# Six attention layers over 128 graphs: new instruction orders around layer 0's result, for the first four groups and at the end

## The chip, the cores and the metric

One Trainium2 chip, of which one core runs the program. The time is device microseconds of one execution. The kernel before took 2340.16 us (median of three runs, 2338.4 to 2341.12); the execution that was profiled took 2338.19 us. Engines: PE is TensorE's matmul side and PEld its weight loads, DVE is VectorE, ACT is ScalarE, POOL is GpSimd, SP is SyncE, which here only issues DMAs.

## The reference

128 graphs of 128 nodes, 256 features a node, and a 0/1 adjacency matrix for each graph, go through six layers:

```python
# layer 0: eight heads of 32
q, k, v = x @ Wq + bq, x @ Wk + bk, x @ Wv + bv
attn = softmax(where(adj == 0, -inf, q @ k.T / sqrt(32)))
x = layernorm(x + (attn @ v) @ Wo + bo) * gamma + beta
# layer 1: one head of 256
attn = softmax(where(adj == 0, -inf, (x @ Wq) @ (x @ Wk).T / sqrt(256)))
x = layernorm(x + (attn @ (x @ Wv)) @ Wo + bo) * gamma + beta
# layers 2 to 5: one head, q and k of width 128
attn = softmax(where(adj == 0, -1e10, (x @ Wq.T + bq) @ (x @ Wk.T + bk).T / sqrt(128)))
x = layernorm(x + (where(adj == 0, 0, attn) @ x) @ Wc.T) * gamma + beta
```

All of it is float32. The output is x after layer 5.

## The kernel before

**Groups, items and slots.** Two graphs are a group; there are 64 groups. One layer (1 to 5) of one group is an item, and the items stand in numbered slots: slot 5g + 4(layer - 1) holds that layer of group g, so from slot 16 on each run of five slots holds one item of each layer, of five different groups. Slot i is written i16, i17 and so on, and a period is five slots. Layer 0 of a group is no item: its parts are spread over the slots ahead of the group's layer 1 by `due(i, lead)`, which gives the group whose layer 1 stands `lead` slots later. With lead 9, 8 and 7 its v, q and k are projected (`project_v0`, `project_q0`, `project_k0`); with 6 all scores are made (`score0`); with 6 to 3 the four units of two heads go through the row minimum (`row_max0`), the exponential (`exp0`), the reciprocal, the scaling on POOL (`normalise_probs0`), the transposing on PE and the move out of PSUM (`move_probs0T`); with 3 the heads are made (`heads0`), with 2 they are split (`move_headsT`, `split_headsT`) and joined (`join_heads`), and the residual and the statistics follow on DVE; with 1 the result is normalised. This result is called GROUP.

**Split operands.** A projection is three float32r products (high by high, high by low, low by high). So ACT writes the high half of a transposed x (`split_hi`), DVE the low half (`split_lo`), and only then can PE run `project_qk` of the item.

**An item.** PE: `transpose_x`, `project_qk`, `project_v` in two halves, `score`, and one slot later `transpose_probs`, two slots later `context`. ACT: `split_hi`, `move_qk`, `softmax`, `move_probsT`, `move_v`. DVE: `split_lo`, `row_max`, then `add_residual`, `statistics` and `normalise` (L1007, two TENSOR_SCALAR). POOL: `find_rstd` (L1172 and L1174), `scale` by gamma (L1190) and `shift` by beta (L1198), which writes the item's x. The first and last few results are `alone`: DVE makes them by itself in `centre` and `finish`, and POOL only gives the reciprocal deviation.

**What sets the order.** The kernel is raw: each engine has its own written program, a loop over the slots with the calls in a fixed order, and semaphores between the engines. Nothing reorders it. An instruction that waits holds all that stands behind it on its engine. ACT's `exp0` of one unit is four ACTIVATEs (L740). After slot 320 an order written out by hand runs the last five items (`LAST_ITEMS`; p, q, a, b, c, d, e are slots 319, 320, 321, 322, 324, 325, 327).

For the item of the layer before, the wait of `transpose_x` is `wait_result`, on `x_ready` (or `alone_ready`); for layer 1 it is GROUP's x. `score` waits for `qk_ready` and for the item before's `probsT_ready`.

## Time and profile before

| what | value |
|---|---|
| median of three runs | 2340.16 us |
| the profiled execution | 2338.19 us, of which its span 2336.4 us |
| PE busy | 2257.7 us, 97% of the span |
| PEld, DVE, ACT, POOL busy | 91%, 76%, 69%, 77% |
| mean granted TensorE clock | 0.994 |

A busy share is an average over stages. Here there are three: the filling of the pipeline (slots -12 to about 15, the first 140 us), the steady part in which a period comes 59 times, and the draining from about 2220 us on. A time in the rows is from the span's start. "Idle before" in brackets is the time the engine stood still before that instruction, with what ended it. PE's own ends are modelled, so two matmuls overlap by some tenths in the rows: a hole in PE is read from the starts, as a distance that is longer than the same distance where nothing waits.

### The profile page before, as it was taken

The numbers are of one execution on the slowest core, as the hardware profiler recorded it, in microseconds if no ns is written. First come the engines' busy times: TensorE is split into PE (matmuls) and PEld (weight loads), VectorE is DVE, ScalarE is ACT, GpSimd is POOL, SyncE is SP. The second block draws the span as 40 slices with busy tenths as digits, with TensorE's granted clock in tenths as the row PEclk, the third lists the DMA queues.
The fourth block names the chain that finished last, engine by engine and source line by source line (L and its number), as shares of the span: only waits on it lengthen the run. The fifth ranks groups of instructions, "written<-read, shape, count | busy, mean of one in ns | idle before, by whom it ended". The sixth has DMA issues, their size and how long they took to land.

```text
span 2336.4 us, 59698 instructions
## 1 busy us (share of the span) xinstructions
PE 2257.7 (97%) x20624; PEld 2132.9 (91%) x20624; DVE 1771.6 (76%) x7736; ACT 1614.4 (69%) x5515; POOL 1787.6 (77%) x2397
## 2 busy tenths in 40 slices
PE   6899999999999999999999999999999999999986
PEld 5799999999999999999999999999999999999985
DVE  4777877877877877777777777777778778777776
ACT  5667767767767767767767767767677677677653
POOL 3368878878878878878788788788788788788762
PEclk9999999999999999999999999999999999999998
DMA  4000110110110110010010100100100100000000
GB/s 157 20 24 24 31 29 24 31 29 24 31 29 24 30 30 24 27 33 22 29 31 24 28 29 26 29 28 27 28 29 26 29 27 28 29 25 26 11 15 14
DMA packets 38747, 68.78 MB, mean 29 GB/s; under 512 B 4400, under 2 KB 12848, under 8 KB 37936
## 3 DMA queue, kind: packets, MB, share of 16 engines
q1 hardware_dynamic: 38448, 64.97, 9.2%
q8 instruction: 166, 2.72, 0.5%
q14 instruction: 133, 1.09, 0.2%
HBM read 48.18 MB, written 16.78 MB: 28 GB/s over the span
## 4 chain that ended last, share of the span: by engine, by line
PE 78%; DVE 9%; ACT 8%; issue 2%; POOL 2%; DMA 0%; POOLq 0%; SPq 0%; DVEq 0%
PE value_bank L464 17%; PE qk_bank L456 16%; PE context_bank L619 9%; PE unit_bank L464 8%; PE unit_bank L456 7%; PE score_bank L603 5%; PE qk_bank L569 5%; ACT probs L740 5%; PE unit_bank L523 5%; PE unit_bank L535 3%; PE score_bank L600 2%; DVE scores L919 2%; PE score_bank L610 2%; DVE xT_lo L948 2%; DVE scores L954 1%
## 5 line engine op out<-in xcount | busy, mean ns | idle before, releaser
L1190 POOL TENSOR_TENSOR x<-y,rows 128x512 f32<-128x512 f32 x304 | 390.3, 1284 | 188.5 <-DVE y L1007 188.5
L740 ACT ACTIVATE probs<-scores,negmax 128x128 f32<-128x128 f32 x1024 | 400.8, 400 | 88.9 <-DVE negmax L919 88.9
L1007 DVE TENSOR_SCALAR y<-y,mv,rstd 128x256 f32<-128x256 f32 x728 | 299.4, 453 | 175.7 <-POOL rstd L1174 175.5
L456 PE MATMUL qk_bank<-xT_hi,w_lo 128*128 128x256 f32 x1280 | 414.9, 324 | 17.0 <-DVE xT_lo L948 13.0
L1198 POOL TENSOR_TENSOR x<-x,rows 128x512 f32<-128x512 f32 x304 | 392.5, 1291 | 19.1
L762 ACT CAST xT_hi<-qk_bank 128x512 fp32r<-128x512 f32 x257 | 150.1, 584 | 355.0 <-PE qk_bank L569 354.9
L464 PE MATMUL value_bank<-w_lo,xT_hi 128*128 128x256 f32 x1280 | 393.7, 308 | 0.0
L456 PE MATMUL qk_bank<-xT_lo,w_hi 128*128 128x256 f32 x1280 | 362.5, 283 | 0.0
L456 PE MATMUL qk_bank<-xT_hi,w_hi 128*128 128x256 f32 x1280 | 360.8, 282 | 0.0
L464 PE MATMUL value_bank<-w_hi,xT_lo 128*128 128x256 f32 x1280 | 360.8, 282 | 0.0
L464 PE MATMUL value_bank<-w_hi,xT_hi 128*128 128x256 f32 x1280 | 358.8, 280 | 0.0
L988 DVE SCALAR_TENSOR_TENSOR y<-context_bank,rtotal,x 128x256 f32<-128x256 f32 x640 | 279.3, 478 | 95.0 <-PE context_bank L619 94.6
L619 PE MATMUL context_bank<-v,probsT 128*128 128x256 f32 x1280 | 336.5, 385 | 1.7 <-ACT probsT L794 1.7
L1179 POOL TENSOR_TENSOR probs<-probs,rtotal 128x256 f32<-128x256 f32 x512 | 307.2, 621 | 37.6 <-DVE rtotal L938 37.6
L788 ACT ACTIVATE probs<-scores,negmax 128x128 f32<-128x128 f32 x640 | 254.4, 404 | 65.7 <-DVE negmax L954 65.6
L1174 POOL TENSOR_TENSOR rstd<-var_eps,minus_half 128x2 f32<-128x2 f32 x384 | 273.0, 711 | 32.0
L456 PEld LDWEIGHTS qk_bank<-xT_hi,w_lo 128*128 128x128 f32 x1280 | 242.5, 189 | 49.7 <-DVE xT_lo L948 37.8
L954 DVE CUSTOM_DVE_ANT_0 scores<-score_bank,mask 128x128 f32<-128x128 f32 x640 | 160.4, 289 | 167.4 <-PE score_bank L603 147.6
L996 DVE BATCH_NORM_STATS2 bn<-y 128x6 f32<-128x256 f32 x768 | 285.6, 414 | 0.0
L456 PEld LDWEIGHTS qk_bank<-xT_hi,w_hi 128*128 128x128 f32 x1280 | 243.2, 190 | 4.8
L464 PEld LDWEIGHTS value_bank<-w_hi,xT_hi 128*128 128x128 f32 x1280 | 243.3, 190 | 0.1
L619 PEld LDWEIGHTS context_bank<-v,probsT 128*128 128x128 f32 x1280 | 218.6, 190 | 26.8 <-ACT probsT L794 2.4
(98 smaller groups left out, 6532.7 us busy)
## 6 DMA issues: line engine op xcount, KB each, us to landing
x0T<-xT_in SPq DMA_DIRECT2D x64, 256.0 KB, 3.0
x<-x_in SPq DMA_DIRECT2D x64, 256.0 KB, 3.1
out<-x_out SPq DMA_DIRECT2D x64, 256.0 KB, 2.3
adj<-adj_in SPq DMA_DIRECT2D x64, 128.0 KB, 2.2
late_weights<-w_in SPq DMA_DIRECT2D x2, 1024.0 KB, 7.3
rows<-rows_in SPq DMA_DIRECT2D x1, 1792.0 KB, 11.6
probs0T<-w_in SPq DMA_DIRECT2D x4, 256.0 KB, 4.1
x<-w_in SPq DMA_DIRECT2D x1, 1024.0 KB, 13.1
```

The lines of the kernel that those rows point to most:

```text
L456: mm = pe.matmul(psum[:, n * G * N:(n + 1) * G * N], split(w, name, kd, at, at + P), flat(xT_half[:, kd]), start=kd == 0 and w is w_lo, st ...
L464: mm = pe.matmul(psum[:, g * D:(g + 1) * D], xT_half[:, kd, g], split(w, name, kd), start=kd == 0 and w is w_lo, stop=kd == KD - 1 and xT_ ...
L619: mm = pe.matmul(context_bank[:, g * D:(g + 1) * D], probsT[:, ring(i), g], v[:, ring(i), g], start=True, stop=True)
L740: e = act.activation(probs0[:, j, g, quad], scores0[:, j, g, quad], ACT.Exp, scale=-1.0, bias=negmax0[:, j, g, quad:quad + 1], accum_out=t ...
L788: e = act.activation(probs[:, ring(i), g], scores[:, ring(i), g], ACT.Exp, scale=-1.0, bias=negmax[:, small(i), g:g + 1], accum_out=total[ ...
L988: dve.scalar_tensor_tensor(y[:, r, g], psum[:, g * D:(g + 1) * D], factor[:, g:g + 1], kept[:, g], ALU.mult, ALU.add).then_inc(y_ready, 1)
L996: last = note(dve.bn_stats(bn[:, r, g], y[:, r, g]))
L1007: m = dve.tensor_scalar(y[:, r, g], y[:, r, g], mv[:, r, g, 0:1], rstd[:, r, g:g + 1], ALU.subtract, ALU.mult)
L1174: pool.tensor_tensor(rstd[:, r], var_eps[:, r], minus_half[:, :], ALU.pow).then_inc(rstd_ready, 1)
L1179: m = pool.tensor_tensor(probs0[:, j, g], probs0[:, j, g], rtotal0[:, j, g].unsqueeze(2).to_broadcast([P, QUADS, N]), ALU.mult)
L1190: pool.tensor_tensor(result(norm), y[:, NORM_AT[norm] % YS], row_of_each(f"gamma{layer}"), ALU.mult).then_inc(zg_ready, 1)
L1198: pool.tensor_tensor(result(norm), result(norm), row_of_each(f"beta{layer}"), ALU.add).then_inc(x_ready, 1)
```

## The change

Seven things are moved or split; apart from how one unit's exponentials are issued (in two halves), no arithmetic is added or removed.

1. DVE, all periods: in the slots with `due(i, 1)` and `due(i, 0)` (i19 and i20, say), the item's `row_max` stands behind `split_lo` (and in the first of them behind GROUP's `normalise`) and not ahead of it.
2. DVE, slot with `due(i, 2)` (i18): GROUP's `add_residual` and `statistics` stand ahead of the normalising of item i-2 and not behind it. POOL, same slot: `find_rstd` of GROUP stands ahead of `scale` of item i-2.
3. ACT: the unit 0 of `exp0` is issued in two halves, the first graph in slot i19, the second at the start of i20.
4. Groups 0 to 3 (`early`): PE makes `transpose_probs0(3)` and `heads0` ahead of the next group's q, and `join_heads` ahead of the next group's k; ACT makes `exp0(2)` and `exp0(3)` a step sooner, ahead of `move_qk`; DVE and POOL follow; the normalising of the item in that slot stands behind `split_headsT`; GROUP's `centre` and `finish` get `row_max0(0)` between them.
5. The fused weights of layer 1 are split one slot later.
6. From i316 on: `score` stands in its own slot, and `context` one slot sooner, behind it.
7. In the order at the end: `transpose_x(e)` ahead of `project_v(d, 0)`, `row_max(e)` ahead of `add_residual(d)`, both last results centred before either is finished, and some neighbours swapped.

```diff
 def scored_early(i):
-    return not item(i + 1) or i >= LAST_FIRST + 3
+    return not item(i + 1) or i > LAST_FIRST
+
+def context_early(i):
+    return i > LAST_FIRST
+
+def early(group):
+    return 0 <= group < 4
...
@@ tensor @@
-                if (group := due(i, 8)) is not None:
+                if (group := due(i, 3)) is not None and early(group):
+                    transpose_probs0(group, 3)
+                if (group := due(i, 8)) is not None and not early(group - 1):
                     project_q0(group)
-                if (group := due(i, 7)) is not None:
+                if (group := due(i, 7)) is not None and not early(group - 1):
                     project_k0(group)
-                if item(i - 2):
+                if item(i - 2) and not context_early(i - 2):
                     context(i - 2)
+                if (group := due(i, 3)) is not None and early(group):
+                    heads0(group)
+                if (group := due(i, 8)) is not None and early(group - 1):
+                    project_q0(group)
                 if item(i):
                     project_qk(i)
...
                 if (group := due(i, 2)) is not None:
                     join_heads(group)
+                if (group := due(i, 7)) is not None and early(group - 1):
+                    project_k0(group)
...
                 if item(i) and scored_early(i):
                     score(i)
+                if item(i - 1) and context_early(i - 1):
+                    context(i - 1)
                 if item(i) and not late_values(i):
                     project_v(i, 1)
...
+            transpose_x(e)
             project_v(d, 0)
-            transpose_x(e)
             score(d)
...
@@ scalar @@
                 if item(i):
                     split_hi(i)
+                if (group := due(i, 5)) is not None and item(i - 1):
+                    exp0(group, 0, [1])
...
                 if (group := due(i, 3)) is not None:
                     move_probs0T(group, 2)
+                    if early(group):
+                        move_probs0T(group, 3)
...
-                if (group := due(i, 6)) is not None:
-                    exp0(group, 0)
+                if (group := due(i, 6)) is not None and not early(group):
+                    exp0(group, 0, [0] if item(i) else range(G))
                 if (group := due(i, 5)) is not None:
                     exp0(group, 1)
+                    if early(group):
+                        exp0(group, 2)
...
@@ vector @@
-                if item(i - 1):
+                urgent = due(i, 1) is not None or due(i, 0) is not None
+                if item(i - 1) and not urgent:
                     row_max(i - 1)
+                if item(i - 2) and context_early(i - 2):
+                    add_residual(("item", i - 2))
                 if item(i):
                     split_lo(i)
-                if (group := due(i, 1)) is not None:
-                    finish_or_normalise(("group", group))
+                if (group := due(i, 1)) is not None and ("group", group) not in ALONE_AT:
+                    normalise(("group", group))
+                if item(i - 1) and urgent:
+                    row_max(i - 1)
                 if (group := due(i, 2)) is not None:
                     split_headsT(group)
+                    if item(i - 3) and early(group):
+                        finish_or_normalise(("item", i - 3))
+                if (group := due(i, 1)) is not None and ("group", group) in ALONE_AT:
+                    centred = centre(("group", group))
                 if (group := due(i, 6)) is not None:
                     row_max0(group, 0)
+                if (group := due(i, 1)) is not None and ("group", group) in ALONE_AT:
+                    finish(("group", group), centred)
...
-                if item(i - 2):
-                    finish_or_normalise(("item", i - 2))
                 if (group := due(i, 2)) is not None:
                     add_residual(("group", group))
                     statistics(("group", group))
+                if item(i - 2) and not (due(i, 3) is not None and early(due(i, 3))):
+                    finish_or_normalise(("item", i - 2))
...
             reciprocal_total(d)
+            row_max(e)
             add_residual(("item", d))
-            row_max(e)
...
@@ gpsimd @@
                 if item(i - 1):
                     keep_valid(i - 1)
+                if (group := due(i, 2)) is not None:
+                    find_rstd(("group", group))
                 if item(i - 2):
                     scale(("item", i - 2))
...
                 if (group := due(i, 2)) is not None:
-                    find_rstd(("group", group))
                     scale(("group", group))
                     shift(("group", group))
```

Three places show how the instructions stand. The first is DVE from GROUP's residual to GROUP's normalising (i18 and the start of i19) in the steady part, before. L988 on `unit_bank` is GROUP's residual, L1007 the normalising (first of item i16, then of GROUP), L954 is `row_max`, L948 `split_lo`.

```order
L1007 TENSOR_SCALAR y<-y,mv,rstd 128x256 x2
L988 SCALAR_TENSOR_TENSOR y<-unit_bank,rvalid,x 128x256 x2
L996 BN_STATS bn<-y 128x6 x2
L999 BN_AGGR mv<-bn 128x2 x2
L954 ISA scores,negmax<-score_bank,mask 128x128
L954 ISA negmax 128x1
L954 ISA scores,negmax<-score_bank,mask 128x128
L954 ISA negmax 128x1
L948 TENSOR_TENSOR xT_lo<-qk_bank,xT_hi 128x512
L1007 TENSOR_SCALAR y<-y,mv,rstd 128x256 x2
```

The same place after the change, where the line numbers are 30 higher:

```order
L1018 SCALAR_TENSOR_TENSOR y<-unit_bank,rvalid,x 128x256 x2
L1026 BN_STATS bn<-y 128x6 x2
L1029 BN_AGGR mv<-bn 128x2 x2
L1037 TENSOR_SCALAR y<-y,mv,rstd 128x256 x2
L978 TENSOR_TENSOR xT_lo<-qk_bank,xT_hi 128x512
L1037 TENSOR_SCALAR y<-y,mv,rstd 128x256 x2
L984 ISA scores,negmax<-score_bank,mask 128x128
L984 ISA negmax 128x1
L984 ISA scores,negmax<-score_bank,mask 128x128
L984 ISA negmax 128x1
```

GROUP's residual and statistics went to the front, the row minimum to the back.

The second is DVE at the step from i19 to i20, before: the normalising of item i17, `row_max` of i19, `split_lo` of i20 (on `unit_bank`), and the first reciprocal of unit 0.

```order
L1007 TENSOR_SCALAR y<-y,mv,rstd 128x256 x2
L954 ISA scores,negmax<-score_bank,mask 128x128
L954 ISA negmax 128x1
L954 ISA scores,negmax<-score_bank,mask 128x128
L954 ISA negmax 128x1
L948 TENSOR_TENSOR xT_lo<-unit_bank,xT_hi 128x512
L938 RECIPROCAL rtotal<-total 128x4
```

And after:

```order
L1037 TENSOR_SCALAR y<-y,mv,rstd 128x256 x2
L978 TENSOR_TENSOR xT_lo<-unit_bank,xT_hi 128x512
L984 ISA scores,negmax<-score_bank,mask 128x128
L984 ISA negmax 128x1
L984 ISA scores,negmax<-score_bank,mask 128x128
L984 ISA negmax 128x1
L968 RECIPROCAL rtotal<-total 128x4
```

`split_lo` stands between item i17's normalising and the row minimum of i19.

The third is POOL in i18 and the start of i19, before. L1172 and L1174 are `find_rstd`, L1190 `scale`, L1198 `shift`; `x_out` is written for an item of layer 5.

```order
L1172 TENSOR_SCALAR var_eps<-mv 128x2
L1174 TENSOR_TENSOR rstd<-var_eps,minus_half 128x2
L1165 TENSOR_TENSOR rtotal<-rtotal,valid 128x2
L1190 TENSOR_TENSOR x_out<-y,rows 128x512
L1172 TENSOR_SCALAR var_eps<-mv 128x2
L1174 TENSOR_TENSOR rstd<-var_eps,minus_half 128x2
L1190 TENSOR_TENSOR x<-y,rows 128x512
L1198 TENSOR_TENSOR x<-x,rows 128x512
```

And after, with line numbers 48 higher:

```order
L1220 TENSOR_SCALAR var_eps<-mv 128x2
L1222 TENSOR_TENSOR rstd<-var_eps,minus_half 128x2
L1213 TENSOR_TENSOR rtotal<-rtotal,valid 128x2
L1220 TENSOR_SCALAR var_eps<-mv 128x2
L1222 TENSOR_TENSOR rstd<-var_eps,minus_half 128x2
L1238 TENSOR_TENSOR x_out<-y,rows 128x512
L1238 TENSOR_TENSOR x<-y,rows 128x512
L1246 TENSOR_TENSOR x<-x,rows 128x512
```

The scaling of item i16 now stands between GROUP's reciprocal deviation and GROUP's own scaling.

## Rows read from the trace of the kernel before

**Rows 1.** The page: busy tenths of PE in 40 slices.

```profile
PE   6899999999999999999999999999999999999986
```

**Rows 2.** Windows: stretch; length; busy of PE, PEld, DVE, ACT, POOL; clock; DMA.

```profile
140.52:175.74 35.22, 34.89 (x324) 33.13 (x324) 26.77 (x123) 25.07 (x87) 27.43 (x38) 1.00 0.08 20
...
2196.00:2336.40 140.40, 116.05 (x903) 103.66 (x902) 97.64 (x368) 69.67 (x219) 68.13 (x102) 0.96 0.03 12
```

**Rows 3.** Waits of PEld, 140 to 2196 us: total, times, longest.

```profile
PEld unit_bank L569 <- POOL x L1198: 19.1, 58, 0.3
PEld qk_bank L456 <- DVE xT_lo L948: 18.9, 59, 1.2
```

**Rows 4.** Timeline of PE, one period: start, us, instruction, idle before.

```profile
165.16 0.28 PE L464 MATMUL unit_bank<-w_hi,headsT_lo 128*128 128x256 f32 x1
...
172.19 0.28 PE L464 MATMUL value_bank<-w_hi,xT_lo 128*128 128x256 f32 x1
172.60 0.66 PE L569 MATMUL unit_bank<-eye,x 128*128 128x128 f32 x4
173.46 0.68 PE L603 MATMUL score_bank<-kT,qT 128*128 128x128 f32 x4 [0.20 <-ACT probsT L794]
...
181.75 0.39 PE L456 MATMUL qk_bank<-xT_hi,w_lo 128*128 128x256 f32 x1
```

**Rows 5.** Timeline of DVE, same period.

```profile
166.19 0.87 DVE L988 SCALAR_TENSOR_TENSOR y<-unit_bank,rvalid,x 128x256 f32<-128x256 f32 x2
...
173.55 0.74 DVE L1007 TENSOR_SCALAR y<-y,mv,rstd 128x256 f32<-128x256 f32 x2 [0.36 <-POOL rstd L1174]
174.20 0.29 DVE L954 CUSTOM_DVE_ANT_0 scores<-score_bank,mask 128x128 f32<-128x128 f32 x1
...
174.62 0.69 DVE L948 TENSOR_TENSOR xT_lo<-unit_bank,xT_hi 128x512 fp32r<-128x512 f32 x1
```

**Rows 6.** Timeline of POOL, same period.

```profile
166.35 1.28 POOL L1190 TENSOR_TENSOR x_out<-y,rows 128x512 f32<-128x512 f32 x1 [0.69 <-DVE y L1007]
168.03 0.22 POOL L1172 TENSOR_SCALAR var_eps<-mv 128x2 f32<-128x2 f32 x1 [0.39 <-DVE mv L999]
168.32 0.71 POOL L1174 TENSOR_TENSOR rstd<-var_eps,minus_half 128x2 f32<-128x2 f32 x1
...
171.26 1.29 POOL L1198 TENSOR_TENSOR x<-x,rows 128x512 f32<-128x512 f32 x1
```

**Rows 7.** Timeline of ACT, same period.

```profile
167.56 0.59 ACT L762 CAST xT_hi<-qk_bank 128x512 fp32r<-128x512 f32 x1 [1.49 <-PE qk_bank L569]
...
174.74 0.40 ACT L788 ACTIVATE probs<-scores,negmax 128x128 f32<-128x128 f32 x1 [0.86 <-DVE negmax L954]
...
180.31 0.58 ACT L762 CAST xT_hi<-qk_bank 128x512 fp32r<-128x512 f32 x1
```

**Rows 8.** Timelines of DVE, POOL and PE where a normalising met a POOL instruction.

```profile
425.99 2.11 DVE L1007 TENSOR_SCALAR y<-y,mv,rstd 128x256 f32<-128x256 f32 x2
...
429.18 0.39 PE L456 MATMUL qk_bank<-xT_hi,w_lo 128*128 128x256 f32 x1 [0.81 <-DVE xT_lo L948]
...
2256.40 1.68 DVE L1007 TENSOR_SCALAR y<-y,mv,rstd 128x256 f32<-128x256 f32 x2 [1.08 <-POOL rstd L1174]
...
2256.33 1.28 POOL L1198 TENSOR_TENSOR x_out<-x_out,rows 128x512 f32<-128x512 f32 x1
```

**Rows 9.** Timelines of PE and ACT while the pipeline fills.

```profile
26.02 0.84 ACT L725 ACTIVATE q0T<-unit_bank,cols 128x256 f32<-128x256 f32 x2 [0.82 <-PE unit_bank L456]
...
73.68 1.13 PE L600 MATMUL score_bank<-xT,qT 128*128 128x128 f32 x8 [1.00 <-ACT probsT L794]
...
89.69 0.39 PE L456 MATMUL qk_bank<-xT_hi,w_lo 128*128 128x256 f32 x1 [2.66 <-DVE xT_lo L948]
```

**Rows 10.** Timeline of PE while it drains.

```profile
2282.08 1.03 PE L619 MATMUL context_bank<-v,probsT 128*128 128x256 f32 x4
2283.64 0.39 PE L456 MATMUL qk_bank<-xT_hi,w_lo 128*128 128x256 f32 x1 [0.54 <-DVE xT_lo L948]
```

More of the change, by code:

```diff
@@ L645, in _ @@
                     project_v0(group)
-                if (group := due(i, 3)) is not None:
+                if (group := due(i, 3)) is not None and not early(group):
                     transpose_probs0(group, 3)
@@ L661, in _ @@
                     transpose_probs0(group, 2)
-                if (group := due(i, 3)) is not None:
+                if (group := due(i, 3)) is not None and not early(group):
                     heads0(group)
@@ L670, in _ @@
             p, q, a, b, c, d, e = LAST_ITEMS
-            context(p)
             project_qk(a)
@@ L734, in move_k0, with exp0 @@
                 m.then_inc(k0_ready, 1)
-            def exp0(group, j):
+            def exp0(group, j, graphs=range(G)):
                 act.wait_ge(negmax0_ready, after_unit(group, j))
-                for g in range(G):
+                for g in graphs:
                     for quad in range(QUADS):
@@ L742, in exp0 @@
                                            accum_out=total0[:, j, g, quad:quad + 1])
-                e.then_inc(exp0_ready, 1)
+                if g == G - 1:
+                    e.then_inc(exp0_ready, 1)
             def move_probs0T(group, j):
@@ L829, in _ @@
                     move_v(i - 1)
-                if (group := due(i, 6)) is not None:
-                    exp0(group, 0)
+                if (group := due(i, 6)) is not None and not early(group):
+                    exp0(group, 0, [0] if item(i) else range(G))
                 if (group := due(i, 5)) is not None:
                     exp0(group, 1)
+                    if early(group):
+                        exp0(group, 2)
                 if (group := due(i, 4)) is not None:
                     move_probs0T(group, 1)
-                    exp0(group, 3)
+                    if not early(group):
+                        exp0(group, 3)
                 if (group := due(i, 8)) is not None:
@@ L844, in _ @@
                     move_probsT(i - 1)
+                if (group := due(i, 6)) is not None and early(group):
+                    exp0(group, 0, [0] if item(i) else range(G))
                 if (group := due(i, 5)) is not None:
-                    exp0(group, 2)
-                if (group := due(i, 3)) is not None:
+                    exp0(group, 3 if early(group) else 2)
+                if (group := due(i, 3)) is not None and not early(group):
                     move_probs0T(group, 3)
-                if i == -5:
+                if i == -4:
                     split_fused(0)
@@ L862, in _ @@
             move_v(a)
+            move_probsT(a)
             split_hi(b)
-            move_probsT(a)
             move_qk(b)
@@ L1072, in _ @@
                     reciprocal0(group, 2)
+                    if early(group):
+                        reciprocal0(group, 3)
                 if item(i - 1) and item(i - 1)[0] == 1:
@@ L1075, in _ @@
                 if item(i - 2):
-                    add_residual(("item", i - 2))
+                    if not context_early(i - 2):
+                        add_residual(("item", i - 2))
                     statistics(("item", i - 2))
@@ L1088, in _ @@
                     find_valid(group)
-                    reciprocal0(group, 3)
+                    if not early(group):
+                        reciprocal0(group, 3)
                 if (group := due(i, 8)) is not None:
                     make_mask(group)
-                if item(i - 2):
-                    finish_or_normalise(("item", i - 2))
                 if (group := due(i, 2)) is not None:
@@ L1107, in _ @@
             row_max(q)
+            add_residual(("item", p))
             split_lo(a)
-            add_residual(("item", p))
             statistics(("item", p))
@@ L1119, in _ @@
             statistics(("item", a))
-            centred = centre(("item", a))
+            normalise_alone(("item", a))
             row_max(b)
-            finish(("item", a), centred)
             split_lo(c)
@@ L1137, in _ @@
             reciprocal_total(d)
+            row_max(e)
             add_residual(("item", d))
-            row_max(e)
             statistics(("item", d))
             reciprocal_total(e)
-            normalise_alone(("item", d))
+            centred_d = centre(("item", d))
             add_residual(("item", e))
             statistics(("item", e))
-            normalise_alone(("item", e))
+            centred_e = centre(("item", e))
+            finish(("item", d), centred_d)
+            finish(("item", e), centred_e)
         @block.gpsimd
@@ L1205, in _ @@
                     normalise_probs0(group, 2)
+                    if early(group):
+                        normalise_probs0(group, 3)
                 if (group := due(i, 3)) is not None:
-                    normalise_probs0(group, 3)
+                    if not early(group):
+                        normalise_probs0(group, 3)
                     make_residual0(group)
```

2 lines of the change are left out of this document (1 added, 1 removed).

## The prediction

> **What bounds the kernel now.** I read the page first. PE is busy in nine tenths of nearly every slice; the holes are in the first three slices and the last one or two [rows 1]. So PE's stream sets the time, and an order can win only PE's idle time. The windows say how much there is: one steady period takes 35.22 us, and the last 140.4 us hold 116.05 us of PE's work, so 24 us of holes [rows 2]. In the steady part the page shows no hole, since matmul ends are modelled; the waits of PEld do. Twice in each of 58 or 59 periods its weight load waits, for x from POOL (19.1 us in all) and for xT_lo from DVE (18.9 us) [rows 3]. The timeline of one period (GROUP 4, items i16 to i21) gives the places, read by starts:
>
> A. The last product ahead of the transpose starts at 172.19, and the next could follow 0.12 later, at 172.31; `transpose_x(i20)` starts at 172.60, because it waits for GROUP's x, whose shift on POOL ran from 171.26 to 172.55 [rows 4, 6]. A hole of 0.29.
> B. `score(i19)` starts 0.86 after that transpose; four transposes take 0.43 where nothing waits. It waits for ACT, which ran unit 0's exponentials ahead of the move. A hole of 0.43.
> C. `project_qk(i21)` at 181.75 waits for `split_lo(i21)`, which waits for `split_hi(i21)` on ACT at 180.31 [rows 4, 7]. By PEld's waits 18.9 / 59 = 0.3.
>
> Together 1.0 us a period, some 59 us in all. Behind C is a chain that I take for the real bound of a period: POOL's deviation of i17, DVE's normalising of i17 (173.55), `row_max(i19)` (174.20), `softmax(i19)` on ACT (174.74), then ACT without a break up to `split_hi(i21)` (180.31), `split_lo`, `project_qk(i21)` [rows 5, 7]. The trace has one test of it: at 425.99 that stretch's normalising took 2.11 us in place of some 1.24, `split_lo` came late, and PE lost 0.81 us at 429.18 in place of 0.3 [rows 8]. What comes late in that chain costs PE its full length.
>
> **The steady part.** Nothing on PE moves. I follow the same period with the new orders.
>
> On DVE, GROUP's residual can start 0.32 after the last join product (165.16, so 165.48; elsewhere in the trace this distance is 0.31 to 0.32) in place of 166.19 [rows 4, 5]. With its statistics it takes 1.75, so it is through at 167.23, not 167.93; i16's normalising follows and ends as late as the old block did, at 167.9. `split_lo(i19)` needs ACT's high half (167.56 + 0.59 = 168.15 [rows 7]), so it runs from 168.2 to 168.85, and GROUP's normalising could start there (before: 169.07).
>
> On POOL, GROUP's `find_rstd` takes 1.0 (168.03 to 168.32 + 0.71) and would end at about 168.3, and now `scale(i16)` follows at once, for 1.28 us, up to 169.6 [rows 6]. GROUP's normalising comes at 168.85 in the middle of it. What happens then is in the trace: at 2256.40 a pair of the same instruction began 0.07 after a POOL instruction of 1.28 us and took 1.68 in place of 0.74 [rows 8]. The longest single one took 1.36. The DVE instruction stood until POOL's was over. So GROUP's normalising ends at about 170.2, not 169.5. POOL's `scale` and `shift` of GROUP then need 2.65, and x is there at 172.9: hole A grows from 0.29 to 0.6.
>
> The Trainium skill has this as a rule (SBUF — State Buffer, section Who interferes with whom): DVE's two-port modes, which `tensor_scalar` can enter, and GpSimd share one pair of ports, and "whoever issues first gets the shared pair for the whole instruction". The trace agrees. By the rule the collision is certain here, since POOL issues first; without it the period would lengthen by 0.6 only, as under the first rival.
>
> Then the chain. All that DVE does after GROUP's normalising is 0.7 later than before (the order inside it costs nothing), so i17's statistics, its deviation and its normalising come 0.7 later: 174.25. Behind it stands now `split_lo(i20)` with a step of 0.65 ahead of `row_max(i19)`, which comes at 174.25 + 0.65 + 0.65 = 175.5 in place of 174.20. So 1.3 later; `softmax(i19)` and ACT's unbroken run keep the 1.3. The two exponentials that moved to the start of i20 lie in ACT's 0.86 of idle time before that softmax and cost nothing; if that cover were gone they would cost 0.8. Hole B shrinks from 0.43 to about 0.1, since only half a unit stands ahead of `move_qk`: but the PE time it frees is given back at C, because the chain does not start from PE. `project_qk(i21)` starts at 183.05, and the period takes 36.5. Behind C nothing else is near: ACT's and DVE's next steps have idle time before them.
>
> Bounds. Below: without the port collision i17's normalising stays at 173.6, `split_lo(i20)` alone shifts `row_max(i19)`, 0.6 a period. The second bound needs more: even with everything else on time, `split_lo(i20)` waits for `transpose_x(i20)` at 172.31 and ACT's half behind it (0.69 + 0.63), so it starts at 173.63 and `row_max(i19)` 0.61 later, at 174.24, as late as now: 0.0. Above: POOL's short `find_rstd` of GROUP meets the two instructions of i16's normalising and loses 0.4, so 1.7. I take 1.3, the value from the row at 2256.40, as the periods are alike. It holds for 59 periods: 59 x 1.3 = +77 us (0.6: +35; 1.7: +100).
>
> **Filling the pipeline (groups 0 to 3).** Gains: normalising items behind `split_headsT` and `split_lo` takes away the waits for xT_lo, 2.66 at 89.69 and one like it a period on (1.96), and the join of group 1 waited 2.24 behind such a `finish`; the first of the three stands in [rows 9]. Together 6.9. Losses: (a) `exp0(2)` stands ahead of `move_qk` of the layer-1 item; `score` of that item waits for ACT already (1.00 at 73.68), and a unit takes 1.55, in groups 1, 2 and 3, of which the sooner `row_max` gives back about half: 2.5. (b) `move_headsT` stands on ACT behind `move_q0`, whose q is now projected behind `heads0`: 1.4 of projection and 0.84 of move [rows 9] before the join can begin, in groups 0 and 1: 2.2 each, of which k's projection had filled 1.5 before. 3.0 in all. Net about -1. Longer holes can also drop PE's clock, which was at its lower level (1.2 GHz) four times in this stretch, each time behind a hole of 2 to 4 us; one more costs about 1.7. Range -7 to +8.
>
> **Draining.** `context` filled PE between the next item's transpose and its projection. That distance is set by ACT's and DVE's halves (2.0 us from the transpose; the context at 2282.08 lay inside it, and `project_qk` at 2283.64 waited all the same) [rows 10]. Now it lies behind `score`, so each of five slots is longer by its 0.67: +3.4. Two slots also take `score` in, with a wait for probsT of 0.5 and its own 0.44 out of the same gap: +1.9. `transpose_x(e)` waits for qk_bank: +0.4. `row_max(e)` a residual sooner: -1.3, and a wait of 0.7 for an x goes. Sum +3.7, range 0 to +8. The fused weights a slot later and the swaps inside this order cost nothing: other work covers them.
>
> **The sum**, against the profiled execution's 2338.2: -1 + 77 + 3.7 = 2417.9; the median of the runs is 2.0 above that execution, so 2420.
>
> **The rivals.**
> 1. *The ports do not collide.* For: some normalisings beside a short POOL instruction were not slowed. Against: the rows at 425.99 and 2256.40. Then 0.6 a period: 2338.2 + 35 + 2.7 + 2 = 2378. Chance 0.17.
> 2. *The other side: A and B shrink and nothing takes their place.* Place: `score(i19)` and `transpose_x(i20)`; price: A 0.25 and B 0.33, 0.58 a period, -34 us; with the ends as above 2309. It decides from the point at which softmax(i19) comes less than 0.3 later, measured from the transpose, than now. For: B is what the split of `exp0` frees, and the page's own waits name A and B. Against: ACT is unbroken from 174.74 to 180.31, and 425.99. Chance 0.12.
> 3. *A draw*: the new order of `row_max` and `split_lo` costs what A and B give, the bound 0.0 above. Then 2338.2 + 2.7 + 2 = 2343. Chance 0.06.
>
> **How the numbers follow.** My forecast (1.3 a period, between 1.0 and 1.7) has 0.65: own range 2395 to 2446. Range: 2368 to 2446, which takes in the first rival and leaves out the other two. A measurement of this kernel tells about 0.2% (4.7 us) from no change. Faster 0.13 (the second rival and a little of the third), same 0.05, slower 0.82.
>
> **What would show it.** Right: a period near 36.5 us by the starts of `score0`; pairs of L1037 (GROUP's) of 1.4 us or more in place of 0.74, beginning inside POOL's L1238 on `x_out`; `project_qk` of the layer-5 item waiting over 1 us for xT_lo, and `score` of the layer-2 item 0.1 or less for probsT; PE's clock unchanged at 1.00 in this part. Wrong: a period of 35.2 or less, or GROUP's normalising undisturbed (first rival if the period is 35.8).

## The result, and the profile after

The changed kernel took 2441.37 us (median of six runs, 2438.95 to 2445.76) against 2340.09 of the kernel before in the same set: ratio 1.0435, 95% interval 1.0421 to 1.0448. It is slower, by 4.4%. The forecast was 2420, own range 2395 to 2446. The profiled span is 2437.1 us against 2336.4.

First the page of the kernel after: span, busy time, busy tenths of PE, granted clock, the chain that ended last.

```profile
span 2437.1 us, 59698 instructions
PE 2306.4 (95%) x20624; PEld 2134.4 (88%) x20624; DVE 1812.7 (74%) x7736; ACT 1622.4 (67%) x5515; POOL 1791.5 (74%) x2397
...
PE   6899999999999999999999999999999999999986
...
PEclk9999999999999999999999999999999999999999
...
PE 56%; POOL 20%; DVE 17%; ACT 4%; issue 2%; DMA 0%; DVEq 0%; POOLq 0%; SPq 0%
```

PE still shows nines [rows 1], so the loss is not seen there; it is seen in the chain, which was 78% PE before, and in the windows: the period from `score0` of group 5 to that of group 6, and the draining (columns as in [rows 2]).

```profile
170.78:207.66 36.88, 35.74 (x323) 33.22 (x322) 27.86 (x120) 25.15 (x87) 28.68 (x39) 1.00 0.09 26
2309.62:2437.13 127.51, 99.62 (x753) 87.35 (x752) 90.23 (x332) 60.41 (x194) 58.72 (x88) 0.97 0.04 13
```

A period takes 36.88 us in place of 35.24 (means over 52 periods, groups 6 to 57), at a clock of 1.00. By the starts of `score0`: group 5 comes 2.9 us late, groups 5 to 63 take 95.2 us more (58 x 1.64), the rest 2.7 more. 2.9 + 95.2 + 2.7 = 100.8, the difference of the spans. So the loss is in the period.

Waits of PEld, 140 to 2190 us, answering [rows 3] (total, times, longest):

```profile
PEld qk_bank L466 <- DVE xT_lo L978: 68.3, 112, 1.2
PEld value_bank L474 <- ACT v L803: 34.3, 56, 0.6
PEld unit_bank L579 <- POOL x L1246: 24.5, 55, 0.5
```

The wait for xT_lo comes twice a period now, and there is a new one, of `project_v` for ACT's move of v. The same period as in [rows 4 to 7], PE:

```profile
175.79 0.66 PE L579 MATMUL unit_bank<-eye,x 128*128 128x128 f32 x4 [0.24 <-POOL x L1246]
176.31 0.68 PE L613 MATMUL score_bank<-kT,qT 128*128 128x128 f32 x4
...
180.74 0.39 PE L474 MATMUL value_bank<-w_lo,xT_hi 128*128 128x256 f32 x1 [0.36 <-ACT v L803]
...
186.22 0.39 PE L466 MATMUL qk_bank<-xT_hi,w_lo 128*128 128x256 f32 x1 [0.53 <-DVE xT_lo L978]
```

`score0` stands 2.88 later than before here; take that off every time. `transpose_x(i20)` then comes 0.31 later than in [rows 4], `score(i19)` 0.03 sooner, `project_qk(i21)` 1.59 later. DVE, POOL and ACT:

```profile
168.35 0.88 DVE L1018 SCALAR_TENSOR_TENSOR y<-unit_bank,rvalid,x 128x256 f32<-128x256 f32 x2 [1.03 <-PE unit_bank L474]
...
171.66 1.34 DVE L1037 TENSOR_SCALAR y<-y,mv,rstd 128x256 f32<-128x256 f32 x2
...
177.06 0.74 DVE L1037 TENSOR_SCALAR y<-y,mv,rstd 128x256 f32<-128x256 f32 x2 [0.25 <-POOL rstd L1222]
177.72 0.69 DVE L978 TENSOR_TENSOR xT_lo<-unit_bank,xT_hi 128x512 fp32r<-128x512 f32 x1
178.32 0.28 DVE L984 CUSTOM_DVE_ANT_0 scores<-score_bank,mask 128x128 f32<-128x128 f32 x1
...
183.24 1.91 DVE L1037 TENSOR_SCALAR y<-y,mv,rstd 128x256 f32<-128x256 f32 x2
...
185.48 0.68 DVE L978 TENSOR_TENSOR xT_lo<-qk_bank,xT_hi 128x512 fp32r<-128x512 f32 x1
```

```profile
171.27 1.27 POOL L1238 TENSOR_TENSOR x_out<-y,rows 128x512 f32<-128x512 f32 x1
...
182.53 1.18 POOL L1227 TENSOR_TENSOR probs<-probs,rtotal 128x256 f32<-128x256 f32 x2
183.67 1.32 POOL L1246 TENSOR_TENSOR x_out<-x_out,rows 128x512 f32<-128x512 f32 x1
```

```profile
178.85 0.40 ACT L808 ACTIVATE probs<-scores,negmax 128x128 f32<-128x128 f32 x1 [1.01 <-DVE negmax L984]
...
184.42 0.58 ACT L782 CAST xT_hi<-qk_bank 128x512 fp32r<-128x512 f32 x1
```

GROUP's pair starts 0.39 into POOL's `scale` of x_out and ends 0.46 behind it. `row_max(i19)` comes at 178.32, 1.24 late; `softmax(i19)` and ACT's unbroken run keep that up to `split_hi(i21)`. And then the pair of item i18 takes 1.91 us. Before, it was this, against these two steps of POOL:

```profile
179.13 1.24 DVE L1007 TENSOR_SCALAR y<-y,mv,rstd 128x256 f32<-128x256 f32 x2
```

```profile
178.99 1.23 POOL L1179 TENSOR_TENSOR probs<-probs,rtotal 128x256 f32<-128x256 f32 x2
180.18 1.31 POOL L1198 TENSOR_TENSOR x_out<-x_out,rows 128x512 f32<-128x512 f32 x1
```

That pair was over 0.19 after the `shift` of x_out began. In the kernel after the pair started 1.23 later, while POOL stood only 0.61 later, and its second half stood for the whole `shift`: it began at 13.00 after `score0`, 0.11 into the `shift`, and ended at 14.37, 0.15 behind it.

### The profile page after: what moved, and what is told of

Its sections match the earlier page's. It is cut to its first block, busy times and chain, and to the rows that moved or that the text cites. A ratio compares the mean times of both kernels' runs of the same rounds, so it can differ in the third digit from the quotient of the medians.

```text
span 2437.1 us, 59698 instructions
## 1 busy us (share of the span) xinstructions
PE 2306.4 (95%) x20624; PEld 2134.4 (88%) x20624; DVE 1812.7 (74%) x7736; ACT 1622.4 (67%) x5515; POOL 1791.5 (74%) x2397
## 4 chain that ended last, share of the span: by engine, by line
PE 56%; POOL 20%; DVE 17%; ACT 4%; issue 2%; DMA 0%; DVEq 0%; POOLq 0%; SPq 0%
PE qk_bank L466 12%; PE value_bank L474 11%; PE unit_bank L474 8%; PE unit_bank L466 7%; POOL probs L1227 6%; DVE y L1037 5%; PE context_bank L629 5%; PE qk_bank L579 4%; POOL rstd L1222 4%; POOL x L1238 3%; POOL x L1246 3%; POOL x_out L1246 3%; DVE xT_lo L978 3%; PE unit_bank L545 3%; PE score_bank L613 2%
## 5 line engine op out<-in xcount | busy, mean ns | idle before, releaser
L466 PE MATMUL qk_bank<-xT_hi,w_lo 128*128 128x256 f32 x1280 | 409.3, 320 | 48.4 <-DVE xT_lo L978 46.0
L1037 DVE TENSOR_SCALAR y<-y,mv,rstd 128x256 f32<-128x256 f32 x728 | 370.3, 550 | 75.7 <-POOL rstd L1222 75.7
L1220 POOL TENSOR_SCALAR var_eps<-mv 128x2 f32<-128x2 f32 x384 | 90.8, 237 | 271.0 <-DVE mv L1029 270.8
L474 PEld LDWEIGHTS value_bank<-w_lo,xT_hi 128*128 128x128 f32 x1280 | 242.7, 190 | 38.7 <-ACT v L803 38.5
```

What stands on the lines that cost most here:

```text
L466: mm = pe.matmul(psum[:, n * G * N:(n + 1) * G * N], split(w, name, kd, at, at + P), flat(xT_half[:, kd]), start=kd == 0 and w is w_lo, st ...
L474: mm = pe.matmul(psum[:, g * D:(g + 1) * D], xT_half[:, kd, g], split(w, name, kd), start=kd == 0 and w is w_lo, stop=kd == KD - 1 and xT_ ...
L1037: m = dve.tensor_scalar(y[:, r, g], y[:, r, g], mv[:, r, g, 0:1], rstd[:, r, g:g + 1], ALU.subtract, ALU.mult)
```

## The experiments

Every kernel keeps the period's order on PE, so means over the same 52 periods can be set side by side. All are worked out from the traces, in us after the start of `score0`; "pair" is start / duration of a normalising. The kernel before measured 2337.67 to 2340.52 us in the sets of runs, so a difference in us between kernels of two sets can be off by 3; periods do not have this.

| kernel | period | GROUP's pair | normalising i17 | row_max(i19) | pair of i18 | split_lo(i21) | project_qk(i21) |
|---|---|---|---|---|---|---|---|
| before | 35.24 | 1.18 / 0.74 | 5.66 | 6.31 | 11.25 / 1.25 | 13.14 | 13.89 |
| after | 36.88 | 0.89 / 1.35 | 6.29 | 7.54 | 12.48 / 1.89 | 14.72 | 15.45 |
| b_part2 | 35.55 | 1.14 / 1.10 | 5.99 | 6.64 | 11.58 / 1.25 | 13.47 | 14.21 |
| b_part1 | 36.55 | 1.18 / 0.73 | 5.98 | 7.23 | 12.16 / 1.90 | 14.40 | 15.14 |
| a_due0 | 35.83 | 0.89 / 1.35 | 6.29 | 6.95 | 11.88 / 1.24 | 13.70 | 14.44 |
| c_xout | 36.41 | 0.89 / 1.35 | 6.30 | 7.55 | 12.49 / 0.93 | 14.26 | 15.00 |
| a_nolock | 37.09 | 0.89 / 1.55 | 6.50 | 7.75 | 12.69 / 1.89 | 14.92 | 15.66 |
| c_rest | 35.16 | 1.17 / 0.74 | 5.66 | 6.31 | 11.25 / 1.24 | 13.06 | 13.80 |
| e_best | 34.57 | other form | 4.06 | 5.66 | 11.11 / 1.20 | 12.48 | 13.22 |

The periods of the five others are 35.23 (b_fill), 35.45 (d_form), 35.52 (d_orders), 35.51 (d_pair) and 35.94 (d_ts).

**Part 2 alone** (b_part2), on the kernel before:

```diff
@@ DVE; POOL likewise: find_rstd of GROUP ahead of scale of item i-2 @@
+                if (group := due(i, 2)) is not None:
+                    add_residual(("group", group))
+                    statistics(("group", group))
                 if item(i - 2):
                     finish_or_normalise(("item", i - 2))
```

> The kernel before, with part 2 alone: on DVE GROUP's residual and statistics ahead of the normalising of item i-2, on POOL find_rstd of GROUP ahead of scale of item i-2. row_max(i18) and split_lo(i19) stay ahead of GROUP's normalising, so it starts at 1.2 after score0 and POOL's scale runs up to 1.8. Theory: the pair takes 1.1 to 1.2 in place of 0.74, and the chain behind it comes 0.4 later, with 0.1 more by the second collision: 0.4 to 0.5 a period, 59 x 0.45 = +27, near 2367 us. Rival (no collision): 2335 to 2340.

2357.16 us, ratio 1.0074 (1.0059 to 1.0089); 0.31 a period. DVE and POOL:

```profile
171.92 1.10 DVE L1007 TENSOR_SCALAR y<-y,mv,rstd 128x256 f32<-128x256 f32 x2
```

```profile
171.28 1.28 POOL L1190 TENSOR_TENSOR x_out<-y,rows 128x512 f32<-128x512 f32 x1
```

The pair starts 0.25 later than in the kernel after and ends at the same moment, 0.46 behind POOL: its length is set by POOL's end. So part 2 loses by the collision it makes, though not the second one (1.25 as before), and less than expected.

**Part 1 alone** (b_part1), on the kernel before:

```diff
-                if item(i - 1):
+                urgent = due(i, 1) is not None or due(i, 0) is not None
+                if item(i - 1) and not urgent:
                     row_max(i - 1)
...
                     finish_or_normalise(("group", group))
+                if item(i - 1) and urgent:
+                    row_max(i - 1)
```

> The kernel before, with part 1 alone: row_max behind split_lo (and behind GROUP's normalising) in the slots with due(i, 1) and due(i, 0). Theory: row_max(i19) comes 0.6 later than before, and item i18's normalising meets POOL's shift of x_out as it does in the kernel after (pair 1.9 in place of 1.25 us): 0.6 + 0.3 = 0.9 a period, 59 x 0.9 = +53, near 2393 us (0.6 alone: 2375). softmax(i18) comes 1.8 later and with it the move of qk: hole B grows from 0.43 to about 1, without a price of its own. Rival (only the blocked normalising costs, the order is free): 2340. Rival (both holes B and C are paid): 2425.

2415.90 us, ratio 1.0326 (1.0309 to 1.0343); 1.31 a period, more than expected: GROUP's pair is undisturbed and still the normalising of i17 comes 0.32 late. `row_max(i18)` had used time in which DVE waited for GROUP's deviation; now it comes on top. 1.31 and 0.31 make 1.62 of the 1.64: the rest of the change has next to no price in the period.

**After, with half of part 1 undone** (a_due0):

```diff
-                urgent = due(i, 1) is not None or due(i, 0) is not None
+                urgent = due(i, 1) is not None
```

> The kernel after, with the row minimum of the item ahead of split_lo again in the slots with due(i, 0) (row_max(i19) ahead of split_lo(i20)); all else as after. Measured: 36.88 us a period against 35.24 before, of which project_qk(i21) is 1.56 late counted from score0. Theory (the late chain is GROUP's blocked normalising 0.63, split_lo ahead of the row minimum 0.61, and a longer second collision at item i18's normalising 0.3): the 0.61 goes, and perhaps 0.1 of the collision, 0.6 to 0.7 a period: 59 x 0.65 = -38 us, near 2403 us, with row_max(i19) at 6.9 after score0 in place of 7.54. Rival (PE waits for ACT, which the split exponentials hold up; the new wait of project_v for v): no change, 2441. Rival (this order is the whole of the loss): back to about 2345.

2379.76 us, ratio to before 1.0171 (1.0156 to 1.0186): 61.6 us back where 38 were expected. `row_max(i19)` is 0.59 sooner as computed, but the pair of i18 falls from 1.89 to 1.24 as well, and `project_qk(i21)` is 1.01 sooner. I had this collision down as a part of 0.1.

**The second collision by itself** (c_xout), on the kernel after:

```diff
@@ POOL (and the list of results in the same order) @@
-                if item(i - 4) and item(i - 4)[0] == LAYERS - 1:
-                    shift(("item", i - 4))
...
                     shift(("item", i - 2))
+                if item(i - 4) and item(i - 4)[0] == LAYERS - 1:
+                    shift(("item", i - 4))
```

> The kernel after, with POOL's shift of a layer-5 result (x_out) behind the scale and shift of the slot's other item instead of ahead of them; nothing else moved. It tests the second collision, the pair of item i18's normalising that takes 1.89 us from 12.48 after score0 and ends 0.16 behind that shift (12.89 to 14.21). Theory (that pair stands behind the shift of x_out and so makes row_max(i20) and split_lo(i21) late): the pair takes 1.1 to 1.3, project_qk(i21) comes 0.4 to 0.5 sooner, 36.4 a period, near 2414 us. Rival (ACT's unbroken run alone sets project_qk(i21)): the pair gets shorter, the period stays 36.9, 2441 us.

2413.58 us, ratio to before 1.0326 (1.0311 to 1.0342): 27.8 us back. DVE's pair of i18 in the same period:

```profile
183.72 0.95 DVE L1037 TENSOR_SCALAR y<-y,mv,rstd 128x256 f32<-128x256 f32 x2
```

Nothing of DVE, ACT or PE was reordered, `row_max(i19)` stands where it stood (7.55), and the period is 0.47 shorter. So 0.47 of the 1.64 hung on one POOL instruction.

**The first collision by another form** (a_nolock), on the kernel after, for GROUP alone:

```diff
@@ DVE, still behind the wait for rstd @@
-  dve.tensor_scalar(y, y, mean, rstd, subtract, mult)
+  dve.scalar_tensor_tensor(y, y, mean, gamma, subtract, mult)
@@ POOL @@
-  pool.tensor_tensor(x, y, gamma, mult)
+  pool.tensor_tensor(x, y, rstd broadcast, mult)
```

> The kernel after, with GROUP's normalising on DVE as a SCALAR_TENSOR_TENSOR, (y - mean) * gamma, that waits for the same semaphore as now, and POOL's scale multiplying by the reciprocal deviation instead of gamma; the order of everything is that of after. Theory (the pair takes 1.35 us because a TENSOR_SCALAR of DVE stands while POOL's scale of the item runs): a pair of SCALAR_TENSOR_TENSOR takes 0.87 wherever the trace has one and does not stand, so the pair takes 0.9, the chain behind it comes 0.45 to 0.5 sooner, 59 x 0.48 = -28 us, near 2413 us. Rival (the ports do not collide, the pair is long for another reason): the pair stays at 1.3 or more, 2441 to 2450 us.

2454.99 us, ratio to before 1.0492 (1.0476 to 1.0507): 13.6 us slower than the kernel after, and my premise was false.

```profile
172.41 1.54 DVE L1043 SCALAR_TENSOR_TENSOR y<-y,mv,rows 128x256 f32<-128x256 f32 x2
```

```profile
172.01 1.27 POOL L1250 TENSOR_TENSOR x_out<-y,rows 128x512 f32<-128x512 f32 x1
174.03 1.04 POOL L1250 TENSOR_TENSOR x<-y,rstd 128x512 f32<-128x512 f32 x1 [0.76 <-DVE y L1043]
```

This form stands for POOL too. The pairs of 0.87 that I had looked at read one operand from PSUM (`context_bank`, `unit_bank`); this one reads both from SBUF. The Trainium skill says it (SBUF — State Buffer, section Who interferes with whom): a DVE instruction with two SBUF inputs contends with a GpSimd instruction that reads SBUF. The trace agrees. The run's numbers (a pair of 1.3 or more, no faster than after) are those that I had given the rival, so by itself it does not tell the two apart; b_part2 and c_xout do.

**Parts 3 to 7 alone** (c_rest): after, with parts 1 and 2 undone.

```diff
-                if item(i - 1) and not urgent:
+                if item(i - 1):
                     row_max(i - 1)
...
-                if (group := due(i, 2)) is not None:
-                    find_rstd(("group", group))
                 if item(i - 2):
                     scale(("item", i - 2))
```

> The kernel after with parts 1 and 2 undone, so parts 3 to 7 alone (unit 0's exponentials in halves, the first four groups, the end). By the runs so far parts 1 and 2 cost 1.31 and 0.31 us a period apart and 1.64 together. Theory: part 3 shortens hole B by 0.34 and C gives it back, since ACT's chain does not start from PE: a period of 35.2, and the ends cost what the two traces showed, +1.5 in the filling and +2.7 in the draining: near 2344 us (2338 to 2350). Rival (a hole that shrinks is won: PE's order is bound by the sum of its holes): 34.9 a period, 2324 us. Rival (the split exponentials hold ACT up, which is what project_v's new wait for v shows): 35.5 a period or more, 2360.

2339.39 us, ratio 1.0011 (1.0002 to 1.0020), less than the 0.2% that a measurement of this kernel tells from no change. Hole B is gone from PEld's waits (23.7 us in 58 times for ACT's kT before), and this is where it went:

```profile
PEld qk_bank L466 <- DVE xT_lo L978: 47.6, 118, 1.3
```

In place of 18.6 us in 58 times it waits twice a period. `score(i19)` comes 0.37 sooner, `project_qk(i20)` at 7.47 as before: its `split_lo(i20)` stands behind `row_max(i19)` and the normalising of i17, which wait for POOL. B is given back, and already at `project_qk(i20)`, not at C.

**Parts 4 and 5 alone** (b_fill), on the kernel before: the lines of the change's diff with `early`, GROUP's `centre` and `finish` for results that are alone, and the fused weights a slot later.

```diff
+                if (group := due(i, 3)) is not None and early(group):
+                    transpose_probs0(group, 3)
...
+                if (group := due(i, 3)) is not None and early(group):
+                    heads0(group)
+                if (group := due(i, 8)) is not None and early(group - 1):
+                    project_q0(group)
```

> The kernel before with parts 4 and 5 alone (the orders of the first four groups, fused weights a slot later). The steady part and the end are those of before. Theory of the prediction: -1 us in all (2337); what the traces with parts 4 and 5 show so far is score0 of group 5 at 170.8 to 174.7 us against 167.9 to 170.8 in those without, so +1 to +5: near 2341 us. Rival (a gain as the shorter waits for xT_lo suggest): 2333.

2339.49 us, ratio 1.0005 (0.9996 to 1.0014): no change. PEld's longest wait for xT_lo up to 170 us stays at 2.8 (2.9 before); PE waits 4.3 us for `split_headsT` (headsT_lo) in place of 2.2, as loss (b) had it. PE's waits for xT_lo in this stretch are 6.8 us in 5 in place of 5.3 in 4, so the gain that was forecast for them is not there.

**A version that follows the chain** (d_form, d_orders, d_pair, d_ts, e_best). If POOL's deviation is what the chain waits for, DVE should not wait for it: the form of a_nolock for every result that is not alone, with a wait for the statistics only. First the form alone, then with part 3 and two orders (GROUP's normalising right behind its statistics; `row_max0(1)` behind `split_lo` of i20):

```diff
@@ d_form: normalise, scale @@
-                dve.wait_ge(rstd_ready, at + 1)
+                dve.wait_ge(stats_ready, at + 1)
...
+                pool.wait_ge(rstd_ready, NORM_AT[norm] + 1)
@@ d_orders, besides: DVE @@
                     statistics(("group", group))
+                    if ("group", group) not in ALONE_AT:
+                        normalise(("group", group))
```

> The kernel before, all orders kept, with every normalising that is not alone in another form: DVE makes (y - mean) * gamma (SCALAR_TENSOR_TENSOR, with a wait for the statistics and none for the reciprocal deviation), POOL multiplies by the reciprocal deviation and adds beta. Theory (POOL's deviation is what makes GROUP's x and the normalising of i17 late): GROUP's residual starts 0.6 sooner, since the item's step ahead of it no longer waits; POOL's scale with a broadcast factor takes 1.04 in place of 1.29 (measured in the first set), x of GROUP is there 0.2 to 0.3 sooner; period 35.0, near 2325 us (2300 to 2345). Rival (the new form stands behind POOL's instructions as TENSOR_SCALAR does, and more often since it comes sooner): 2340 or slower.

2349.93 us, ratio 1.0055 (1.0039 to 1.0072). Hole A halves (`transpose_x(i20)` at 4.56, not 4.70), but unit 0's `row_max0` comes 0.10 later, hole B grows by 0.24 (1.10 from transpose to score in place of 0.86), and the pair of i18 stands longer (1.47).

> The same new form of normalising on the kernel before, with part 3 (unit 0's exponentials in halves) and two orders on DVE: GROUP's (y - mean) * gamma right behind its statistics, ahead of row_max and split_lo of the next slot, and row_max0 of unit 1 behind split_lo of the next slot, so that it is not ahead of row_max(i19). Theory: GROUP's x is there 1 us or more sooner (hole A gone), row_max(i19) starts when score(i19) ends (B down by 0.34), project_qk(i21) 0.3 to 0.5 sooner (C gone): a period of 34.4 to 34.6, near 2296 us (2285 to 2320). Rival (collisions of the new form with POOL take it back): 2335 to 2350.

2352.82 us, ratio 1.0068 (1.0053 to 1.0083). `row_max(i19)` at 5.66 and holes A and C gone, as expected, and a new hole eats it, 0.93 us by the starts:

```profile
182.25 0.66 PE L523 MATMUL unit_bank<-eye,probs 128*128 128x128 f32 x4 [0.77 <-POOL probs L1187]
```

**d_pair** put `reciprocal0(0)` ahead of `row_max0(1)`, `split_lo(i21)` ahead of `row_max(i20)`, and x_out's shift later as in c_xout; **d_ts** is the same in the old form, with GROUP's normalising where it was. DVE:

```diff
-                if item(i - 1):
+                if item(i - 1) and not (item(i) and due(i, 4) is not None):
                     row_max(i - 1)
                 if item(i):
                     split_lo(i)
+                if item(i - 1) and item(i) and due(i, 4) is not None:
+                    row_max(i - 1)
...
                     reciprocal0(group, 0)
+                    if item(i - 1):
+                        row_max0(group, 1)
                     row_max0(group, 2)
```

> The kernel with the new form of normalising and its orders (d_orders: 35.52 us a period) with three more orders. Its trace shows the holes A and C gone and one new of 0.93 us, where transpose_probs0 of unit 1 waits for POOL's normalise_probs0, which had waited for the reciprocal of unit 0 that stood on DVE behind row_max0 of unit 1. So: reciprocal0(0) ahead of row_max0(1); split_lo(i21) ahead of row_max(i20); POOL's shift of x_out behind the slot's other scale and shift. Theory: the new hole goes, a period of 34.6 to 34.9 (A, B and C as good as gone), near 2310 us (2295 to 2325). Rival (ACT's unbroken run still sets project_qk(i21), whatever the order on DVE): 35.3 or more, 2340.

2351.41 us, ratio 1.0056 (1.0042 to 1.0070), with a period of 35.51, in the rival's range but not for its reason: the hole stayed at 0.93. I had named the wrong waiter. POOL:

```profile
178.60 0.22 POOL L1182 TENSOR_SCALAR var_eps<-mv 128x2 f32<-128x2 f32 x1 [0.91 <-DVE mv L1002]
...
179.58 1.50 POOL L1189 TENSOR_TENSOR probs<-probs,rtotal 128x256 f32<-128x256 f32 x2
```

`normalise_probs0(1)` stands behind `find_rstd(i18)`, whose statistics stand on DVE behind two `row_max0`.

> The kernel before with its own form of normalising (TENSOR_SCALAR with the reciprocal deviation) and the same orders as far as they apply: unit 0's exponentials in halves, row_max0(1) behind reciprocal0(0) in the next slot, split_lo(i21) ahead of row_max(i20), POOL's shift of x_out later. It tells what the orders give without the new form. Theory (C is split_lo(i21) behind row_max(i20); A is POOL's chain and stays): 0.25 to 0.35 a period of C, 34.9 to 35.0, near 2322 us (2312 to 2332). Rival (the form does it all): 35.2, 2337.

2379.87 us, ratio 1.0176 (1.0161 to 1.0192), a miss by 58 us: here the same statistics come at 10.52 in place of 9.68, and PE waits 0.77 at the same transposes (1.66 in place of 0.89). C did close (context to `project_qk(i21)` 0.68 in place of 0.95) and it was worth nothing.

e_best moves `row_max0(2)` behind those statistics:

```diff
                 if (group := due(i, 5)) is not None:
                     reciprocal0(group, 0)
-                    row_max0(group, 2)
...
                     statistics(("item", i - 2))
+                if (group := due(i, 5)) is not None:
+                    row_max0(group, 2)
```

> d_pair with one more order on DVE: row_max0 of unit 2 behind the residual and the statistics of item i18 instead of ahead of them. d_pair's trace: the hole of 0.93 us stayed, because POOL's normalise_probs0(1) stands behind find_rstd(i18), which waited up to 10.28 for statistics that stood on DVE behind two row_max0. Theory (holes are closed one at a time only when the chain behind them is followed to its first late step): statistics(i18) are there 0.85 sooner, normalise_probs0(1) starts at 10.3 in place of 11.25, the hole goes; a new one of 0.1 to 0.2 at split_lo(i21); period 34.7, with the end 3 us shorter as in d_pair near 2304 us (2296 to 2318). Rival (ACT's exponential of unit 2, at 10.31, comes to wait for row_max0(2) and makes split_hi(i21) late): 35.2 or more, 2335 or slower.

2297.66 us, ratio 0.9822 (0.9809 to 0.9835): 1.8% faster than before, 5.9% than after. The new hole is gone and PEld's waits for x and kT with it; what is left is

```profile
PEld qk_bank L456 <- DVE xT_lo L951: 16.9, 60, 0.3
```

and a period (168.12 to 202.66) of 34.54 us, 34.54 of them PE busy at clock 1.00 (its ends are modelled; by the starts 0.23 of C is left):

```profile
168.12:202.66 34.54, 34.54 (x323) 33.08 (x322) 27.59 (x121) 25.09 (x87) 28.88 (x38) 1.00 0.10 29
```

## Why the prediction was right, and the term that was mis-sized

**The direction and the chain: right.** Lateness of `row_max(i19)` was forecast at 1.3 and is 1.23; it passed through `softmax(i19)` and ACT to `split_hi(i21)` undiminished; `score(i19)` waits under 0.1; the clock is 1.00.

**Its first 0.7: right in sum, wrong in parts.** "GROUP's normalising ends at about 170.2, not 169.5": 170.2 was right (2.24 after `score0`, so 170.14), but before the pair ended at 169.82, so the collision costs 0.32. The 0.7 was counted from 169.5, where the pair would have ended undisturbed with the new order, and not from where it ended before. The other 0.31 of lateness is `row_max(i18)` behind GROUP's normalising, which the prediction had at nothing ("the order inside it costs nothing"); b_part2 and b_part1 show one each. So 0.38 too much and 0.31 too little made the right sum, which was luck. The pair itself took 1.35, under the 1.4 that I had set as the sign. `split_lo(i20)` ahead of `row_max(i19)`: forecast 0.6, measured 0.60.

**The step that failed in size: "Behind C nothing else is near".** A second collision lay 0.6 us away: the pair of i18, 1.25 before, 1.89 after. Of its 0.64, DVE's wait for the scores had hidden 0.2. `split_lo(i21)` is 1.58 late where ACT's run is 1.23, 0.35 more; c_xout prices it at 0.47 a period (there the pair falls to 0.93, below what it was before). That takes the period from a forecast of 36.5 to 36.88. The upper bound of 1.7 held, for another reason than the one given for it: GROUP's `find_rstd` beside i16's normalising took 1.11 in place of 1.00, and not 0.4 more.

**Where PE pays.** I expected over 1 us in front of `project_qk(i21)`. It is 1.57 - 0.68 = 0.89 by the starts (0.27 before); 0.62 is paid already at `project_v(i20)`, whose bank waits for ACT's late move of v, and 0.23 at `project_qk(i20)`. Other holes grow by 0.19 where PE transposes i18's probabilities, 0.13 at A and 0.16 ahead of `transpose_x(i21)`, and B gives back 0.33; together this is 1.6 of the 1.64. Where PE pays does not change the sum at `project_qk(i21)`: ACT's run and, behind it, the pair of i18 set that.

**The ends.** Draining: forecast +3.7, measured +2.7 (c_rest +3.0). Filling: forecast -1; b_fill gives +0.8 with an interval that holds 0, and the profiled execution +2.9. The forecast of -1 is not refuted; gains and losses in this stretch cancel within what can be measured. b_part2, which leaves parts 4 and 5 out, also reaches group 5 at 170.78, so the 2.9 of the one profiled execution need not come from them.

**The sum again.** 2338.2 + 2.9 + 95.2 + 2.7 = 2439.0, and the median lies 2.4 above. Of the 21 us that the forecast missed, 18 are the steady term (95.2 for 77).

**The rivals.** No collision: out by b_part2 and c_xout. A and B win: out, A grew (`transpose_x(i20)` 0.31 later), and c_rest, which has B's gain without parts 1 and 2, is no faster. A draw: out.

## What to carry to other kernels

A hole in the bounding engine is worth nothing until the chain behind it is followed to the first step that is late anyway: closing B alone (c_rest), or B and C (d_ts), gave nothing, and the time came back as a wait elsewhere on PE (`project_qk(i20)` in c_rest, unit 1's transposes in d_orders, d_pair and d_ts), until one order put item i18's statistics, from which POOL's late chain started, ahead of a `row_max0` (e_best). When DVE work moves by half a microsecond, list every POOL instruction that reads SBUF within that reach of every DVE instruction that can stand for it, not only the one at the place of the change. And an instruction placed in a wait that exists anyway is free; the same one behind the wait is not (`row_max(i18)`, ahead of and behind DVE's wait for GROUP's deviation).

## What the runs showed of the hardware

- A TENSOR_SCALAR on DVE (both tensors in SBUF) that began while POOL ran its `scale`, `shift` or product of the probabilities ended 0.15 us behind that POOL instruction, whenever it began. A pair of them then ended 0.46 to 0.48 behind it where POOL did not go on at once: 1.35 and 1.10 us long for starts 0.25 apart, 0.74 alone. Where POOL's next instruction had begun first, the second of the pair stood for that one too (1.89, after).
- SCALAR_TENSOR_TENSOR with both operands in SBUF stands as well (1.55 for 0.87), with one in PSUM it did not (pairs of 0.86 to 0.88 in all kernels; before, 205 single ones began and ended inside a long POOL instruction and took 0.47 to 0.49). It works the other way too: POOL's 0.22 us step on `var_eps` took 0.51 beside such a pair in e_best:

```profile
172.18 0.88 DVE L1011 SCALAR_TENSOR_TENSOR y<-y,mv,rows 128x256 f32<-128x256 f32 x2
```

```profile
172.23 0.51 POOL L1183 TENSOR_SCALAR var_eps<-mv 128x2 f32<-128x2 f32 x1 [0.75 <-DVE mv L1002]
```

- POOL's product of 128x512 with a factor broadcast over the row took 1.04 us, with a full second operand 1.28.
